# A recommendation tower's gathers, each with a wait of its own, and both gram fills of a tile in a row

## Chip, cores and metric

The kernel runs on one core of a Trainium2 chip. The metric is the device time of one execution in microseconds (us), smaller is better. Engines are named as in the profile: PE (TensorE matmul), PEld (TensorE weight load), DVE (VectorE), ACT (ScalarE), POOL (GpSimd), SP (SyncE).

## What is computed

2048 samples, 26 embedding tables of 128 columns, a dense vector of 128 columns. In short, cut from the reference:

```python
e = jnp.stack([tbl_0[ids[:, 0]], ..., tbl_25[ids[:, 25]]], axis=1)     # 2048 x 26 x 128
sd = jnp.einsum('bfd,bd->bf', e, dense)                                # 26 dots with the dense vector
ss = jnp.einsum('bfd,bgd->bfg', e, e)                                  # all pairs of features
z = jnp.concatenate([dense, sd, ss[:, iu, ju]], axis=1)                # upper triangle: 325 pairs
h = jnp.concatenate([z, dense], axis=1)
h = jnp.maximum(h @ W_top1 + b_top1, 0.0)                              # 607 -> 512
h = jnp.maximum(h @ W_top2 + b_top2, 0.0)                              # 512 -> 256
y = h @ W_top3                                                         # 256 -> 1
```

All in fp32.

## The kernel before, in words

The batch is cut into 16 tiles of 128 samples; two tiles make a step `d` of 256 samples, so there are 8 steps. For each tile the kernel needs `vecT`: for every sample its 27 vectors (26 looked up, 1 dense), with the 128 columns on the partitions. They come from two places.

**Tables that PE looks up.** Nine small tables (a tenth in three of the steps) are held in SBUF, split into two fp32r parts. PE spreads the ids (`spread_ids`, L576), DVE compares them with row numbers and so makes a one-hot "pack" (`set_pack`, L356; two packs for a table, a ring of six), and PE multiplies each pack with the table (`lookup`, L602, 8 matmuls a pack). ACT drains the sum into `vecT` (L428). `pack_done` counts packs that PE has finished: 150 in all.

**Tables that are gathered.** The other 17 (16 in the steps with ten lookups) come by POOL's indirect DMAs (L321), 128 rows each, 266 in all, in groups of four a tile, into `rows`, which holds two tiles. PE transposes a group (`transpose_rows`, L615) into one of two PSUM banks `vec_bank`, ACT copies it to `vecT` (L436). `vec_filled` counts what PE has put into `vec_bank`: row groups and gram fills alike.

**The gram.** For each sample PE multiplies its 26 vectors with its 26 vectors (`gram`, L629): two fills of `vec_bank` a tile (h = 0, 1), each 64 matmuls of 26 columns, which the profile records as 128 matmuls and 128 weight loads. ACT drains each fill (L445). DVE turns the result (L366, L372), PE transposes it (L643), ACT drains it (L452). Then comes the tower: layer 1 (L650, L654), layer 2 (L663), layer 3 (L669), one step of 256 samples at a time, in units that are drained by ACT (L460, L471).

The order on PE is written out by hand. In tiles 0 to 13, at the head of a tile, it is: gram fill 0, a unit of layer 1 or 2 of the step before, one pack of the next step's lookups, gram fill 1, another unit, another pack; then the other packs, with the row groups of the next tile between them. `gram` waits, for h = 0, for the last lookup sum, the dense vectors and the last row group of its tile. Tiles 14 and 15 are written out at the end of the program. ACT's program has the same order for its drains.

POOL's gathers of a group wait until the rows that they replace were transposed (`vec_filled`) and, from group 3 on, until the gram fills of the tile two before are done. On top of these, `gate_on_packs` (L306) makes every second gather or so wait for `pack_done`, from a small table of "packs ahead". In tile 1 and after, such waits stand on 9 gathers of a tile.

Of the kernel before, what the change touches and what calls it, by code (L numbers as in the profile page):

```python
# [19 lines left out]
TEN_STEPS = [3, 5, 7]  # L20
LATE_SPLIT = 4
GRAM_AHEAD_OF = 3
FIRST_PACKS_AHEAD = [{8: 1, 10: 2, 12: 3, 14: 4, 16: 5}, {0: 6, 2: 9, 4: 11, 6: 14, 8: 15, 10: 18, 12: 18, 14: 19, 16: 20}]
PACKS_AHEAD = [{0: 2, 2: 4, 4: 5, 6: 7, 8: 8, 10: 9, 12: 9, 14: 10, 16: 10},
               {0: 11, 2: 13, 4: 15, 6: 17, 8: 18, 10: 18, 12: 18, 14: 19, 16: 19}]
SPLIT_AT_FIRST = len(LOOKED_UP) - LATE_SPLIT


# [33 lines left out]
def build(nc, dense_t, ids, ids_t, tables, weights, y):  # L62
# [3 lines left out]
    TD = 2  # L66
# [18 lines left out]
    FG = 4  # L85
# [70 lines left out]
    def group(j):  # L156
        return GATHERED[FG * j:FG * (j + 1)]
# [4 lines left out]
    with ctx:  # L162
# [6 lines left out]
        def sem(name):  # L169
            return ctx.enter_context(nc.semaphore(name))  # L170
# [77 lines left out]
        vec_filled, vec_drained = sem("vec_filled"), sem("vec_drained")  # L248
# [6 lines left out]
        pack_set, pack_done = sem("pack_set"), sem("pack_done")  # L255
# [40 lines left out]
        @block.gpsimd  # L296
        def _(pool):
            nc.gpsimd.memset(ident[:], 0.0).then_inc(ident_zero, 1)
            for c in heights:
                nc.gpsimd.iota(row_i[c][:], pattern=[[1, c]], base=0, channel_multiplier=c  # L300
                               ).then_inc(rows_numbered, 1)
            pool.wait_ge(ident_zero, 1)
            nc.gpsimd.affine_select(out=ident[:], in_=ident[:], compare_op=ALU.not_equal, fill=1.0, base=0,
                                    pattern=[[-1, P]], channel_multiplier=1).then_inc(ident_set, 1)

            def gate_on_packs(tile, n):  # L306
                ahead = (FIRST_PACKS_AHEAD if tile < TD else PACKS_AHEAD)[tile % TD].get(n, 0)
                packs = pack_at(tile // TD, 0) + ahead
                if ahead:
                    pool.wait_ge(pack_done, packs)  # L310

            pool.wait_ge(ids_loaded, 16)
            for tile in range(TILES):
                for j in range(groups(tile)):
                    if tile >= TD:
                        pool.wait_ge(vec_filled, rows_at(same_rows(tile, j)[-1], j) + 1)
                    if tile >= TD and j == GRAM_AHEAD_OF:
                        pool.wait_ge(vec_filled, gram_at(tile - TD, 1) + 1)
                    for n, f in enumerate(group(j)):
# [82 lines left out]
        def _(act):  # L402
# [37 lines left out]
            def drain_gram(tile, h):  # L440
                use = gram_at(tile, h)
                if h == 0 and tile:
                    act.wait_ge(tile_turned, tile)
                act.wait_ge(vec_filled, use + 1)
                nc.scalar.copy(dots[:, h * HALF:(h + 1) * HALF, :],  # L445
                               vec_bank[use % 2][:, 0:HALF * GC].rearrange("p (i f) -> p i f", f=GC)
                               ).then_inc(vec_drained, 1)
# [15 lines left out]
            def drain_layer1(d, m):  # L463
                drain_unit(layer1_at(d, m), h1, m, b1_sb, 0, DS)

            def drain_layer2(d, m):
                drain_unit(layer2_at(d, m), h2, m, b2_sb, 0, DS)

            def drain_y(use, d, t0, nt):
                act.wait_ge(work_filled, use + 1)  # L470
                nc.scalar.copy(y_by_tile[:, TD * d + t0:TD * d + t0 + nt, :],  # L471
                               work_bank[use % 2][:, 0:nt * BL].rearrange("p (t i) -> p t i", t=nt)
                               ).then_inc(work_drained, 1)
# [21 lines left out]

            for tile in range(TILES - 2):
                d, t = tile // TD, tile % TD
                for h in range(2):
                    drain_gram(tile, h)
                    if t == 0 and d:  # L500
                        drain_layer1(d - 1, 1 + h)
                    if t == 1 and d and h == 0:
                        drain_layer2(d - 1, 1)
                    if t == 1 and d and h == 1:
                        drain_y(layer3_at(d - 1), d - 1, 0, TD)
                    drain_table(d + 1, half_packs(d + 1) * t + h)
# [62 lines left out]
        def _(pe):  # L569
# [49 lines left out]
            def gram(tile, h):  # L619
                into = gram_at(tile, h)  # L620
                if h == 0:
                    pe.wait_ge(sum_drained, sum_at(tile // TD + 1, 0))
                    pe.wait_ge(x_copied, tile // TD + 1)
                    pe.wait_ge(vec_drained, rows_at(tile, groups(tile) - 1) + 1)
                free_vec(into)
                for i in range(HALF):
                    for j in range(4):
                        s = BL * j + h * HALF + i
                        last = nc.tensor.matmul(vec_bank[into % 2][BL * j:BL * j + GC, i * GC:(i + 1) * GC],  # L629
                                                vecT[:, slot(tile), s, 0:GC], vecT[:, slot(tile), s, 1:VECS],  # L630
                                                start=True, stop=True)
                last.then_inc(vec_filled, 1)
# [70 lines left out]

            for tile in range(TILES - 2):
                d, t = tile // TD, tile % TD
                for h in range(2):
                    gram(tile, h)
                    if t == 0 and d:
                        layer1(d - 1, 1 + h)
                    if t == 1 and d and h == 0:  # L710
                        layer2(d - 1, 1)
                    if t == 1 and d and h == 1:
                        layer3(d - 1)
                    table_step(d + 1, half_packs(d + 1) * t + h)
                for k in range(2, half_packs(d + 1)):
                    table_step(d + 1, half_packs(d + 1) * t + k)
                    if k in ROWS_AFTER and ROWS_AFTER[k] < groups(tile + 1):
                        transpose_rows(tile + 1, ROWS_AFTER[k])
                    if t == 0 and d and k == LATE_LAYER1_AFTER:
                        layer1(d - 1, M1 - 1)  # L720
                    if k == PAIRS_AFTER:
                        transpose_pairs(tile)
                if t == 0 and d:
                    layer2(d - 1, 0)
                if t == 1:
                    if d == 0:
                        pe.wait_ge(w1x_summed, 1)
                    layer1(d, 0)
# [100 lines left out]
```

## Time and profile before

| | |
|---|---|
| median of 3 runs | 369.99 us (368.86 to 370.70) |
| the profiled execution | 371.11 us, of which the span of the profile is 369.3 us |
| granted TensorE clock, mean | 0.991 |
| PE / PEld busy | 343.2 / 313.1 us |
| DVE / ACT / POOL busy | 230.5 / 189.4 / 257.5 us |
| DMA | 26.85 MB, 73 GB/s on the mean |

A row of the timeline merges instructions of one kind that follow each other: start in us, duration in us, engine, line, operation, tiles, shape, count, and in brackets the idle time of the engine before it with what ended it. "issue" is idle time in which the engine waited for nothing that the profile shows.

### The profile page before, as it was taken

The numbers are of one execution on the slowest core, as the hardware profiler recorded it, in microseconds if no ns is written. First come the engines' busy times: TensorE is split into PE (matmuls) and PEld (weight loads), VectorE is DVE, ScalarE is ACT, GpSimd is POOL, SyncE is SP. The second block draws the span as 40 slices with busy tenths as digits, with TensorE's granted clock in tenths as the row PEclk, the third lists the DMA queues.
The fourth block names the chain that finished last, engine by engine and source line by source line (L and its number), as shares of the span: only waits on it lengthen the run. The fifth ranks groups of instructions, "written<-read, shape, count | busy, mean of one in ns | idle before, by whom it ended". The sixth has DMA issues, their size and how long they took to land.

```text
span 369.3 us, 13778 instructions
## 1 busy us (share of the span) xinstructions
PE 343.2 (93%) x6224; PEld 313.1 (85%) x6224; DVE 230.5 (62%) x324; ACT 189.4 (51%) x283; POOL 257.5 (70%) x273
## 2 busy tenths in 40 slices
PE   2997878999999999999999999999989999999976
PEld 1887768989989898989989898888979889898875
DVE  5798888866839294774849294693928468342030
ACT  1386774544637264644637265453736347372723
POOL 5788777777777777777777777777777777777000
PEclk9998998999999999999999999999999999999999
DMA  7993253222222222222222222222221222222000
GB/s 207 257 236 86 60 179 134 56 52 59 66 58 54 53 73 52 57 56 53 71 54 55 57 67 58 54 53 59 64 60 52 55 60 63 60 52 53 7 5 2
DMA packets 11756, 26.85 MB, mean 73 GB/s; under 512 B 4652, under 2 KB 5804, under 8 KB 11570
## 3 DMA queue, kind: packets, MB, share of 16 engines
q0 software_dynamic: 8512, 17.45, 18.8%
q1 hardware_dynamic: 3186, 8.52, 8.2%
q8 instruction: 49, 0.80, 1.0%
q14 instruction: 9, 0.07, 0.1%
HBM read 25.95 MB, written 0.01 MB: 70 GB/s over the span
## 4 chain that ended last, share of the span: by engine, by line
PE 86%; issue 4%; DMA 4%; POOL 2%; ACT 2%; DVE 1%; SPq 0%; ACTq 0%
PE sum_bank L602 35%; PE vec_bank L629 14%; PE work L654 11%; PE vec_bank L615 7%; PE work L663 7%; PE work L650 4%; POOL rows L321 2%; PE id_bank L576 2%; DMA rows<-in_tbl,ids_all 2%; DMA w_all<-in_tbl 2%; PE work L643 2%; PE sum_bank L598 1%; PE work L739 1%; PE work L669 1%; DVE onehot L356 1%
## 5 line engine op out<-in xcount | busy, mean ns | idle before, releaser
L321 POOL DMA_INDIRECT rows<-in_tbl,ids_all x266 | 256.7, 965 | 82.8 <-issue 68.9
L356 DVE TENSOR_TENSOR onehot<-id_bank,row_f 125x1024 fp32r<-125x1024 f32 x150 | 174.5, 1215 | 91.8 <-PE sum_bank L602 48.3
L602 PE MATMUL sum_bank<-onehot,parts 125*128 125x256 f32 x1152 | 168.1, 292 | 0.3 <-issue 0.3
L602 PEld LDWEIGHTS sum_bank<-onehot,parts 125*128 125x128 f32 x1152 | 151.3, 192 | 4.0 <-issue 0.7
L436 ACT COPY vecT<-vec_bank 128x512 f32<-128x512 f32 (+1 forms) x74 | 84.8, 1149 | 19.0 <-PE vec_bank L615 18.6
L428 ACT COPY vecT<-sum_bank 128x256 f32<-128x256 f32 x75 | 52.3, 697 | 41.0 <-PE sum_bank L602 27.9
L629 PE MATMUL vec_bank<-vecT 128*26 128x26 f32 x4096 | 53.3, 192 | 7.8 <-issue 2.6
L629 PEld LDWEIGHTS vec_bank<-vecT 128*26 128x26 f32 x4096 | 43.9, 103 | 19.5 <-issue 14.4
L460 ACT ACTIVATE late<-work,w_all 128x256 f32<-128x256 f32 (+1 forms) x50 | 22.8, 457 | 50.4 <-PE work L654 30.7
L445 ACT COPY late<-vec_bank 128x416 f32<-128x416 f32 x32 | 16.2, 506 | 58.5 <-PE vec_bank L629 58.5
L366 DVE STREAM_TRANSPOSE late<-late 128x832 f32<-128x832 f32 x16 | 29.4, 1838 | 25.4 <-ACT late L445 25.4
L615 PE MATMUL vec_bank<-ident,rows 128*128 128x128 f32 x266 | 42.3, 278 | 2.8 <-DMA rows<-in_tbl,ids_all 2.8
L654 PE MATMUL work<-late,w_all 126*128 126x256 f32 (+1 forms) x192 | 44.2, 366 | 0.0
L654 PEld LDWEIGHTS work<-late,w_all 126*128 126x128 f32 x192 | 34.8, 190 | 4.5
L615 PEld LDWEIGHTS vec_bank<-ident,rows 128*128 128x128 f32 x266 | 31.8, 142 | 3.6 <-DMA rows<-in_tbl,ids_all 3.2
L663 PE MATMUL work<-late,w_all 128*128 128x256 f32 x112 | 27.1, 386 | 0.3 <-ACT late L460 0.2
L663 PEld LDWEIGHTS work<-late,w_all 128*128 128x128 f32 x112 | 20.2, 189 | 3.5 <-issue 0.7
L576 PE MATMUL id_bank<-idsT,pick 128*128 128x512 f32 x38 | 18.4, 491 | 4.6 <-DVE idsT L380 4.6
L650 PE MATMUL work<-xT,w_all 128*128 128x256 f32 (+1 forms) x64 | 19.9, 392 | 0.2
L372 DVE COPY late<-late 128x6 f32<-128x6 f32 (+2 forms) x144 | 16.5, 198 | 1.5
L598 PE MATMUL sum_bank<-onehot,w_all 125*128 125x256 f32 x48 | 12.4, 416 | 2.5 <-DMA w_all<-in_tbl 2.5
L598 PEld LDWEIGHTS sum_bank<-onehot,w_all 125*128 125x128 f32 x48 | 10.0, 213 | 4.7 <-issue 3.2
(40 smaller groups left out, 104.3 us busy)
## 6 DMA issues: line engine op xcount, KB each, us to landing
rows<-in_tbl,ids_all POOLq DMA_INDIRECT x266, 2.6
late<-in_tbl SPq DMA_DIRECT2D x7, 480.0 KB
w_all<-in_weights SPq DMA_DIRECT2D x1, 1571.0 KB, 7.5
w_all<-in_tbl SPq DMA_DIRECT2D x3, 480.0 KB
xT<-in_dense_t SPq DMA_DIRECT2D x8, 128.0 KB
vecT<-in_ids_t SPq DMA_DIRECT2D x1, 256.0 KB, 2.8
late<-in_weights SPq DMA_DIRECT2D x1, 256.0 KB, 7.8
ids_all<-in_ids SPq DMA_DIRECT2D x1, 208.0 KB, 2.4
```

What stands on the lines that cost most here:

```text
L321: nc.gpsimd.indirect_dma_start(rows[:, tile % TD, FG * j + n, :], None, tables[f], bass.IndirectOffsetOnAxis(ids_all[:, tile, f:f + 1], 0) ...
L356: nc.vector.tensor_tensor(onehot[:, use % RING, 0:width, :], bass.AP(got.tensor, got.offset, [got.ap[0], [0, width], [1, DS]]), bass.AP(nu ...
L366: nc.vector.transpose(turned.rearrange("p c i -> p (c i)"), dots.rearrange("p i c -> p c i")).then_inc(tile_turned, 1)
L428: nc.scalar.copy(step_vec(d, place(LOOKED_UP[n] + 1)), sum_bank[use % 2][:, 0:DS].rearrange("p (t s) -> p t s", t=TD)).then_inc(sum_draine ...
L436: nc.scalar.copy(vecT[:, slot(tile), :, spot:spot + n].rearrange("d s v -> d v s"), vec_bank[use % 2][:, 0:n * P].rearrange("d (v s) -> d ...
L598: last = nc.tensor.matmul(into_sum, uncut[n - SPLIT_AT_FIRST][:, (c0 + c) * DIM:(c0 + c + 1) * DIM], hot.bitcast(fp32), start=first, stop= ...
L602: last = nc.tensor.matmul(into_sum, parts[:, k, CH_AT[n] + c0 + c, :], hot, start=first and k == 0, stop=final and k == PARTS - 1)
L615: last = nc.tensor.transpose(vec_bank[into % 2][:, n * P:(n + 1) * P], rows[:, tile % TD, FG * j + n, :], ident[:])
L629: last = nc.tensor.matmul(vec_bank[into % 2][BL * j:BL * j + GC, i * GC:(i + 1) * GC], vecT[:, slot(tile), s, 0:GC], vecT[:, slot(tile), s ...
L650: nc.tensor.matmul(out, w1x[:, cols], xT[:, d % 2, s0:s0 + ns], start=True, stop=False)
L654: last = nc.tensor.matmul(out, w1p[:, b, cols], pairsT[0:KP, b, s0:s0 + ns], start=False, stop=(b == KT - 1))
L663: last = nc.tensor.matmul(work_bank[use % 2][:, 0:ns], w2_sb[:, b, m * P:(m + 1) * P], h1[:, b, s0:s0 + ns], start=(b == 0), stop=(b == M1 ...
```

## The change

`gate_on_packs` and its two small tables go. In their place stands `GATES`, one entry for each of the 266 gathers: the counter (`PACKS` is `pack_done`, `FILLS` is `vec_filled`) and the value that it waits for, empty for the first eight. And in tiles 0 to 13 both gram fills, and both of their drains, stand directly behind each other at the tile's head.

```diff
-FIRST_PACKS_AHEAD = [{8: 1, 10: 2, 12: 3, 14: 4, 16: 5}, {0: 6, 2: 9, 4: 11, 6: 14, 8: 15, 10: 18, 12: 18, 14: 19, 16: 20}]
-PACKS_AHEAD = [{0: 2, 2: 4, 4: 5, 6: 7, 8: 8, 10: 9, 12: 9, 14: 10, 16: 10},
-               {0: 11, 2: 13, 4: 15, 6: 17, 8: 18, 10: 18, 12: 18, 14: 19, 16: 19}]
+PACKS, FILLS = 0, 1
+GATES = [
...
+    [(FILLS, 23), (FILLS, 24), (PACKS, 43), (PACKS, 44), (PACKS, 45), (FILLS, 26), (FILLS, 26), (FILLS, 27),
+     (FILLS, 27), (FILLS, 27), (PACKS, 46), (FILLS, 28), (PACKS, 47), (PACKS, 48), (PACKS, 49), (FILLS, 30),
+     (PACKS, 51)],
...
+]
...
-            def gate_on_packs(tile, n):
-                ahead = (FIRST_PACKS_AHEAD if tile < TD else PACKS_AHEAD)[tile % TD].get(n, 0)
-                packs = pack_at(tile // TD, 0) + ahead
-                if ahead:
-                    pool.wait_ge(pack_done, packs)
+            def keep_behind_pe(what=None, count=0):
+                if count:
+                    pool.wait_ge([pack_done, vec_filled][what], count)
...
-                        gate_on_packs(tile, FG * j + n)
+                        keep_behind_pe(*GATES[tile][FG * j + n])
...
             for tile in range(TILES - 2):
                 d, t = tile // TD, tile % TD
+                drain_gram(tile, 0)
+                drain_gram(tile, 1)
                 for h in range(2):
-                    drain_gram(tile, h)
...
             for tile in range(TILES - 2):
                 d, t = tile // TD, tile % TD
+                gram(tile, 0)
+                gram(tile, 1)
                 for h in range(2):
-                    gram(tile, h)
```

What the change moves on PE, at the head of tile 3, where units of layer 2 (L663) and layer 3 (L669) of the step before stand between the gram fills (L629; L602 is a pack's lookup, L615 the last row group). Before:

```order
L602 MATMUL sum_bank<-onehot,parts 128x256 x8
L615 MATMUL vec_bank<-ident,rows 128x128
L663 MATMUL work<-late,w_all 128x256 x4
L629 MATMUL vec_bank<-vecT 26x26 x64
L663 MATMUL work<-late,w_all 128x256 x4
L602 MATMUL sum_bank<-onehot,parts 128x256 x8
L629 MATMUL vec_bank<-vecT 26x26 x64
L669 MATMUL work<-late,w_all 32x64 x8
L602 MATMUL sum_bank<-onehot,parts 128x256 x8
```

With the change (L646 is the lookup, L659 the row group, L707 layer 2, L673 the gram, L713 layer 3):

```order
L646 MATMUL sum_bank<-onehot,parts 128x256 x8
L659 MATMUL vec_bank<-ident,rows 128x128
L707 MATMUL work<-late,w_all 128x256 x4
L673 MATMUL vec_bank<-vecT 26x26 x128
L707 MATMUL work<-late,w_all 128x256 x4
L646 MATMUL sum_bank<-onehot,parts 128x256 x8
L713 MATMUL work<-late,w_all 32x64 x8
L646 MATMUL sum_bank<-onehot,parts 128x256 x8
```

Nothing is added or left out on PE; the second fill now comes ahead of a unit and a pack.

On POOL, the first nine gathers of tile 4 with the semaphores that they wait for. Before, every second one waits:

```order
L321 DMA rows<-in_tbl_1,ids_all 128x128 [waits pack_done,vec_filled]
L321 DMA rows<-in_tbl_2,ids_all 128x128
L321 DMA rows<-in_tbl_3,ids_all 128x128 [waits pack_done]
L321 DMA rows<-in_tbl_5,ids_all 128x128
L321 DMA rows<-in_tbl_8,ids_all 128x128 [waits pack_done,vec_filled]
L321 DMA rows<-in_tbl_11,ids_all 128x128
L321 DMA rows<-in_tbl_12,ids_all 128x128 [waits pack_done]
L321 DMA rows<-in_tbl_13,ids_all 128x128
L321 DMA rows<-in_tbl_14,ids_all 128x128 [waits pack_done,vec_filled]
```

With the change each of them does, on whichever counter its entry names:

```order
L364 DMA rows<-in_tbl_1,ids_all 128x128 [waits vec_filled]
L364 DMA rows<-in_tbl_2,ids_all 128x128 [waits vec_filled]
L364 DMA rows<-in_tbl_3,ids_all 128x128 [waits pack_done]
L364 DMA rows<-in_tbl_5,ids_all 128x128 [waits pack_done]
L364 DMA rows<-in_tbl_8,ids_all 128x128 [waits pack_done,vec_filled]
L364 DMA rows<-in_tbl_11,ids_all 128x128 [waits vec_filled]
L364 DMA rows<-in_tbl_12,ids_all 128x128 [waits vec_filled]
L364 DMA rows<-in_tbl_13,ids_all 128x128 [waits vec_filled]
L364 DMA rows<-in_tbl_14,ids_all 128x128 [waits vec_filled]
```

The order of the gathers is the same; their waits are.

## Rows read from the trace of the kernel before

**Rows 1.** The page: busy time, share of the span, instructions, of PE, PEld and POOL

```profile
PE 343.2 (93%) x6224; PEld 313.1 (85%) x6224; DVE 230.5 (62%) x324; ACT 189.4 (51%) x283; POOL 257.5 (70%) x273
```

**Rows 2.** The page: the chain that ended last, by engine

```profile
PE 86%; issue 4%; DMA 4%; POOL 2%; ACT 2%; DVE 1%; SPq 0%; ACTq 0%
```

**Rows 3.** The page's groups: busy, mean ns of one, idle before and what ended it

```profile
L321 POOL DMA_INDIRECT rows<-in_tbl,ids_all x266 | 256.7, 965 | 82.8 <-issue 68.9
...
L629 PE MATMUL vec_bank<-vecT 128*26 128x26 f32 x4096 | 53.3, 192 | 7.8 <-issue 2.6
```

**Rows 4.** Waits: engine, line, releaser; us in total, times, longest

```profile
POOL rows L321 <- PE sum_bank L602: 8.2, 27, 0.3
...
PEld vec_bank L629 <- issue: 14.4, 51, 1.3
```

**Rows 5.** The page: PE's instruction queue; packets, MB, share

```profile
q8 instruction: 49, 0.80, 1.0%
```

**Rows 6.** Timeline of PEld, tile 15's gram fills and what follows

```profile
350.33 1.18 PEld L629 LDWEIGHTS vec_bank<-vecT 128*26 128x26 f32 x128 [0.37 <-issue]
351.54 0.30 PEld L650 LDWEIGHTS work<-xT,w_all 128*128 128x128 f32 x2
351.76 0.75 PEld L654 LDWEIGHTS work<-late,w_all 126*128 126x128 f32 x6
352.63 0.21 PEld L629 LDWEIGHTS vec_bank<-vecT 128*26 128x26 f32 x17
354.03 1.01 PEld L629 LDWEIGHTS vec_bank<-vecT 128*26 128x26 f32 x111 [1.20 <-issue]
355.08 0.30 PEld L650 LDWEIGHTS work<-xT,w_all 128*128 128x128 f32 x2
355.30 0.75 PEld L654 LDWEIGHTS work<-late,w_all 126*128 126x128 f32 x6
355.97 0.53 PEld L774 LDWEIGHTS sum_bank<-xT,w_all 128*128 128x128 f32 x4
356.42 0.53 PEld L774 LDWEIGHTS id_bank<-xT,w_all 128*128 128x128 f32 x4
356.87 0.19 PEld L739 LDWEIGHTS work<-late,w_all 128*128 128x128 f32 x1
357.94 0.86 PEld L739 LDWEIGHTS work<-late,w_all 128*128 128x128 f32 x7 [0.89 <-issue]
```

**Rows 7.** Windows there: busy (count) by engine, PEclk, DMA share, GB/s last

```profile
351.30:351.60 0.30, 0.30 (x38) 0.26 (x25) 0.00 (x0) 0.00 (x0) 0.00 (x0) 1.00 0.00 0
351.60:352.10 0.50, 0.50 (x6) 0.50 (x6) 0.00 (x0) 0.38 (x1) 0.00 (x0) 1.00 0.12 33
...
355.10:355.60 0.50, 0.50 (x10) 0.50 (x5) 0.00 (x0) 0.39 (x1) 0.00 (x0) 1.00 0.16 33
```

**Rows 8.** Timeline of PE, head of tile 3

```profile
100.35 1.71 PE L629 MATMUL vec_bank<-vecT 128*26 128x26 f32 x128
102.00 1.99 PE L663 MATMUL work<-late,w_all 128*128 128x256 f32 x8
103.64 1.30 PE L602 MATMUL sum_bank<-onehot,parts 125*128 125x256 f32 x8
104.87 2.02 PE L629 MATMUL vec_bank<-vecT 128*26 128x26 f32 x128
106.70 0.46 PE L669 MATMUL work<-late,w_all 128*32 128x64 f32 x16
```

**Rows 9.** Timeline of PEld, long idle times near fills in tiles 1, 11 and 12

```profile
65.56 0.61 PEld L629 LDWEIGHTS vec_bank<-vecT 128*26 128x26 f32 x63 [0.64 <-issue]
...
276.25 0.26 PEld L669 LDWEIGHTS work<-late,w_all 128*32 128x32 f32 x12 [0.83 <-issue]
...
296.00 0.30 PEld L650 LDWEIGHTS work<-xT,w_all 128*128 128x128 f32 x2 [1.01 <-issue]
```

**Rows 10.** Timeline: POOL's last gather of tile 6; PEld, the transposes that need it

```profile
155.21 0.94 POOL L321 DMA_INDIRECT rows<-in_tbl,ids_all  x1 [0.30 <-issue]
...
158.19 0.47 PEld L615 LDWEIGHTS vec_bank<-ident,rows 128*128 128x128 f32 x4
```

**Rows 11.** Timeline: POOL's eleventh gather of tile 4; time to landing of all gathers

```profile
106.53 0.94 POOL L321 DMA_INDIRECT rows<-in_tbl,ids_all  x1 [0.30 <-issue]
...
DMA to landing us min/median/max: 2.4/2.6/6.5
```

**Rows 12.** Timeline: the table copies of tile 0 on ACT and DVE, and PE's wait behind them

```profile
42.76 1.02 ACT L415 COPY work<-w_all 125x1024 f32<-125x1024 f32 x1
...
49.19 1.23 DVE L341 TENSOR_TENSOR parts<-work,parts 125x1024 fp32r<-125x1024 f32 x1 [0.91 <-ACT parts L409]
...
55.47 0.85 PE L643 MATMUL work<-ident,late 128*126 128x128 f32 x3 [2.60 <-DVE late L372]
```

**Rows 13.** Windows: columns as in Rows 7

```profile
50.00:55.00 5.00, 2.88 (x24) 2.59 (x21) 4.97 (x11) 3.41 (x5) 3.78 (x5) 1.00 0.77 244
55.00:60.00 5.00, 4.53 (x24) 4.35 (x24) 5.00 (x9) 2.22 (x4) 3.78 (x5) 0.66 0.62 236
...
350.00:355.00 5.00, 3.70 (x266) 3.32 (x264) 0.00 (x0) 1.43 (x5) 0.00 (x0) 1.00 0.01 3
```

More of the change, by code:

```diff
@@ L22 @@
 GRAM_AHEAD_OF = 3
-FIRST_PACKS_AHEAD = [{8: 1, 10: 2, 12: 3, 14: 4, 16: 5}, {0: 6, 2: 9, 4: 11, 6: 14, 8: 15, 10: 18, 12: 18, 14: 19, 16: 20}]
-PACKS_AHEAD = [{0: 2, 2: 4, 4: 5, 6: 7, 8: 8, 10: 9, 12: 9, 14: 10, 16: 10},
-               {0: 11, 2: 13, 4: 15, 6: 17, 8: 18, 10: 18, 12: 18, 14: 19, 16: 19}]
+PACKS, FILLS = 0, 1
+GATES = [
+    [(), (), (), (), (), (), (), (), (PACKS, 1), (PACKS, 1), (PACKS, 2), (PACKS, 3), (PACKS, 3), (FILLS, 1),
+     (PACKS, 5), (PACKS, 6), (FILLS, 2)],
+    [(PACKS, 9), (FILLS, 3), (PACKS, 12), (PACKS, 13), (FILLS, 4), (PACKS, 15), (PACKS, 16), (PACKS, 17),
+     (PACKS, 18), (PACKS, 18), (FILLS, 6), (PACKS, 19), (PACKS, 19), (FILLS, 7), (PACKS, 20), (FILLS, 8),
+     (PACKS, 23)],
+    [(FILLS, 9), (FILLS, 10), (PACKS, 25), (PACKS, 25), (PACKS, 25), (PACKS, 25), (PACKS, 26), (FILLS, 11),
+     (FILLS, 12), (FILLS, 12), (FILLS, 13), (PACKS, 28), (PACKS, 28), (FILLS, 14), (PACKS, 30), (PACKS, 31),
+     (PACKS, 32)],
+    [(PACKS, 33), (FILLS, 17), (PACKS, 34), (FILLS, 18), (FILLS, 19), (FILLS, 19), (FILLS, 19), (FILLS, 20),
+     (FILLS, 20), (PACKS, 37), (FILLS, 21), (FILLS, 21), (FILLS, 21), (PACKS, 39), (FILLS, 22), (PACKS, 40),
+     (PACKS, 40)],
+    [(FILLS, 23), (FILLS, 24), (PACKS, 43), (PACKS, 44), (PACKS, 45), (FILLS, 26), (FILLS, 26), (FILLS, 27),
+     (FILLS, 27), (FILLS, 27), (PACKS, 46), (FILLS, 28), (PACKS, 47), (PACKS, 48), (PACKS, 49), (FILLS, 30),
+     (PACKS, 51)],
+    [(FILLS, 31), (PACKS, 52), (FILLS, 32), (FILLS, 33), (FILLS, 33), (FILLS, 33), (FILLS, 34), (FILLS, 34),
+     (PACKS, 55), (PACKS, 55), (FILLS, 35), (FILLS, 35), (PACKS, 56), (FILLS, 36), (PACKS, 58), (PACKS, 58),
+     (FILLS, 37)],
+    [(PACKS, 60), (PACKS, 61), (PACKS, 62), (FILLS, 39), (FILLS, 40), (PACKS, 64), (PACKS, 64), (FILLS, 41),
+     (FILLS, 41), (FILLS, 41), (PACKS, 65), (FILLS, 42), (PACKS, 66), (FILLS, 43), (PACKS, 68), (FILLS, 44)],
+    [(PACKS, 70), (PACKS, 71), (PACKS, 71), (FILLS, 46), (PACKS, 74), (PACKS, 74), (PACKS, 74), (FILLS, 47),
+     (FILLS, 47), (PACKS, 75), (PACKS, 75), (FILLS, 48), (FILLS, 48), (PACKS, 76), (FILLS, 49), (PACKS, 78)],
+    [(PACKS, 78), (PACKS, 79), (FILLS, 50), (FILLS, 51), (PACKS, 81), (FILLS, 52), (PACKS, 83), (PACKS, 83),
+     (PACKS, 83), (FILLS, 53), (FILLS, 53), (PACKS, 84), (PACKS, 84), (FILLS, 54), (PACKS, 86), (FILLS, 55),
+     (PACKS, 87)],
+    [(FILLS, 56), (FILLS, 57), (PACKS, 90), (FILLS, 58), (FILLS, 59), (FILLS, 59), (FILLS, 59), (FILLS, 60),
+     (FILLS, 60), (PACKS, 93), (PACKS, 93), (FILLS, 61), (FILLS, 61), (PACKS, 94), (FILLS, 62), (PACKS, 96),
+     (PACKS, 96)],
+    [(PACKS, 97), (PACKS, 98), (FILLS, 64), (PACKS, 99), (FILLS, 65), (FILLS, 66), (PACKS, 102),
+     (PACKS, 102), (FILLS, 67), (FILLS, 67), (FILLS, 67), (PACKS, 103), (FILLS, 68), (FILLS, 68),
+     (PACKS, 104), (FILLS, 69)],
+    [(PACKS, 106), (FILLS, 70), (FILLS, 71), (PACKS, 109), (FILLS, 72), (PACKS, 111), (PACKS, 112),
+     (PACKS, 112), (PACKS, 112), (FILLS, 73), (FILLS, 73), (PACKS, 113), (FILLS, 74), (FILLS, 74),
+     (FILLS, 74), (PACKS, 114)],
+    [(FILLS, 75), (PACKS, 116), (PACKS, 116), (FILLS, 76), (FILLS, 77), (PACKS, 119), (PACKS, 119),
+     (FILLS, 78), (PACKS, 121), (PACKS, 121), (FILLS, 79), (FILLS, 79), (FILLS, 79), (PACKS, 122),
+     (FILLS, 80), (FILLS, 80), (PACKS, 123)],
+    [(FILLS, 81), (PACKS, 125), (FILLS, 82), (FILLS, 83), (PACKS, 128), (PACKS, 129), (PACKS, 130),
+     (FILLS, 85), (FILLS, 85), (FILLS, 86), (FILLS, 86), (FILLS, 86), (PACKS, 131), (PACKS, 131),
+     (FILLS, 87), (FILLS, 87), (PACKS, 132)],
+    [(FILLS, 88), (PACKS, 134), (PACKS, 134), (PACKS, 135), (PACKS, 136), (FILLS, 90), (PACKS, 137),
+     (FILLS, 91), (FILLS, 92), (PACKS, 140), (PACKS, 140), (PACKS, 140), (FILLS, 93), (FILLS, 93),
+     (PACKS, 141), (FILLS, 94)],
+    [(FILLS, 94), (PACKS, 143), (FILLS, 95), (PACKS, 145), (FILLS, 96), (FILLS, 97), (PACKS, 147),
+     (FILLS, 98), (PACKS, 149), (PACKS, 150), (PACKS, 150), (FILLS, 99), (FILLS, 99), (FILLS, 99),
+     (FILLS, 100), (FILLS, 100)],
+]
```

## The prediction

> **What bounds the kernel now.** I read the page first. PE is busy 343.2 of 369.3 us [rows 1], and 86% of the chain that ended last is PE's [rows 2]: what lengthens PE's work lengthens the kernel, nearly one for one. Then the groups and the waits. POOL is a steady stream, 0.94 us busy and 0.30 us between gathers, and none of its waits on PE is over 0.3 us [rows 3, 4], which is the same 0.30 that stands ahead of a gather without a wait: no gate holds it today. The row to look at is a third one: PEld idled 14.4 us in 51 places inside the gram, "issue", the longest 1.3 us [rows 4]. Nothing that the profile shows held it there, so I went for PE's own instructions.
>
> PE and PEld record 6224 + 6224 = 12448 instructions [rows 1]; PE's instruction queue brought 49 packets, 0.80 MB [rows 5], one for 254 of them (256 with the waits between). A gram fill is 128 matmuls and 128 loads, so **one fill eats one packet**. Tile 15 shows what that does, because the gathers are over by then and the only transfers are instructions. Its first fill starts at 350.33 [rows 6]; transfers are at zero until 351.60, then 33 GB/s for 0.5 us, which is one packet of 16 KB [rows 7]; 17 loads into the second fill PEld stops for 1.20 us and goes on at 354.03 [rows 6], 2.4 us after the packet began. From there 111 + 2 + 6 + 4 + 4 + 1 = 128 loads pass, with their matmuls 256 instructions, and it stops again, 0.89 us, until 357.94 [rows 6]; that packet came in the window from 355.10 [rows 7]. So a packet is asked for about 1.1 to 1.3 us after the last border is crossed, is there some 2.5 us later, and two borders crossed at full speed cannot lie closer than 3.7 to 3.9 us.
>
> Elsewhere PE keeps clear of this, since between the two fills stand a unit and a pack: in tile 3 the second fill starts 4.5 us after the first [rows 8]. The stall shows only where a border falls badly: 0.64, 0.83, 1.01 us [rows 9], and twice smaller (0.26 and 0.48 us by the same view).
>
> **The gram fills, the large term.** 14 tiles now run 512 instructions without a pause. Such a stretch holds exactly two borders, 256 instructions or one fill's time apart, today 1.65 us [rows 8]. The second must wait for its packet. Tile 15 gives the length: from the first fill's start to the go-on 3.7 us; without the unit between, the border would lie 25 loads into the second fill, 103 loads remain, and at the 1.67 us of a mean fill (53.3 / 32, [rows 3]) these are 1.3 us: 5.0 us for the pair. Where the border lies later, the packet is asked for later and less remains, so I take 4.9 for all. Today a pair takes 1.65 + 1.83 = 3.5 us [rows 8], 3.4 on the mean. Plus 1.5 us by 14 is **+21.0**. The five stalls of today in these tiles go with it, 0.64 + 0.83 + 1.01 + 0.26 + 0.48: **-3.2**. One entry into and one exit from the small shape are saved a tile; no row has two fills in a row. The first fill shows 0.37 us idle ahead of its loads, most of it after a drain [rows 6], which would be 14 x 0.37 = 5.2 at most, and 0 at least; in tile 3 PE shows no idle time ahead of either fill [rows 8], so I take **-1.0**. In tile 13 the count puts the first border at the very head of the pair, hence a third one right behind its end, 1.7 us after the go-on where 3.7 are needed: **+2.0**.
>
> Here a rule speaks against me. The Trainium skill ("Runtime: NRT & Kernel Launch", Instruction fetch mechanics) gives PE's instruction memory as 2048 instructions, refilled in blocks of 256 while the current one runs, the cost of a border mostly hidden. By that a burst of 512 would be covered and this whole term would be zero. It also calls the memory two lines of one block each, which is what tile 15 looks like; the two sentences disagree, and [rows 6] decide for the second.
>
> **Behind the fills.** In tile 0 ACT's copy of a table, at 42.76 us, moves behind the drain of the second fill, some 2.9 us later; DVE waits for it (0.91 us already) and PE for DVE, 2.60 us [rows 12]. PE itself comes 1.5 later, so its wait grows by what is over, less DVE's slack: **+0.4**. In the other tiles ACT has each fill drained in 0.5 us, and the units behind wait for nothing new: 0.
>
> **The gates.** A gather's new event lies 0.35 to 3.9 us before its start in the order of today, so with the old order they would bind nowhere. The move spoils some: gather 11 of tile 4 starts at 106.53 [rows 11] and waits for pack 46, the one at the head of tile 3, whose matmuls end at 103.64 + 1.30 = 104.94 [rows 8]; this pack now stands behind the second fill, 1.7 us later in PE's order before any stall. POOL then slips up to 1 us, a tile or so at a time, and since its stream has no reserve (17 x 1.25 = 21.2 us a tile, as PE's), what it loses counts where the margin is small, at the row groups that PE transposes. That is tiles 4 and 6: the last gather of tile 6 starts at 155.21, lands 2.6 us later [rows 11], 157.8, and the transposes start at 158.19 [rows 10]: 0.4 us. I take 0.5 us at each, **+1.0**. Bounds: 0 (the stalls slow PE and give POOL time), and 3 if four tiles have it at 0.75 each. The waits themselves cost nothing, since the 0.30 us ahead of a gather are there with and without one [rows 3, 4]. Behind a gather's wait stand only gathers, so PE's transposes are the only ones who can feel it.
>
> **The clock.** In the 5 us after PE's 2.60 us wait in tile 0 the granted clock is 0.66; after tile 15's 1.20 us stall it stays at 1.00 [rows 13]. The new stalls, 1.3 to 2.3 us, lie between. A stretch at 0.66 loses (1 - 0.66) x 5 = 1.7 us at most, none where PE is held by instructions. Ends: 0, and 14 x 1.7 = 24. Nearest is the row at 1.20, so I take little, **+2.0**.
>
> Sum: 21.0 - 3.2 - 1.0 + 2.0 + 0.4 + 1.0 + 2.0 = 22.2. The profiled execution took 371.1; 393.3 then, and 1.1 less against the median of the runs: **392 us**.
>
> **Rivals.** (A) PE fetches further ahead than tile 15 makes me think (there the program's end is near): the stalls do not come, only the gates' 1.0 and tile 0's 0.4 are left, 371.4 us. The rule above says so; for it, most of the 49 borders pass unseen; against it, the stops exactly 256 instructions apart. 0.08. (B) Faster: the fills gain by their neighbourhood. Nothing stalls, the entry is saved, 14 x 0.37 = 5.2, and the 3.2 of today go: 371.1 - 8.4 + 1.4 - 1.1 = 363 us. It decides if a packet is there within 1.65 us of the one before; tile 15's took 3.7. 0.05. (C) The clock drops behind half of the stalls or more: 14 x 1.7 / 2 = 12 in place of 2, 402 us, and 414 if behind all. 0.15. (D) No stalls, but the gates bind: their 3 us with tile 0's 0.4, 373 us. 0.04. My forecast has 0.68, with a range of its own from 384 to 399: a pair between 4.4 and 5.3 us.
>
> **Numbers.** Half a per cent is about what a measurement of this kernel can tell from no change. Slower: 0.68 + 0.15 + 0.04 = 0.87; within half a per cent, A: 0.08; faster, B: 0.05. The range runs from 380 to 406: it holds the forecast and most of C, and leaves out A, B, D (0.17) and the far end of C. Its lower end is a pair at 4.1 us in place of 4.9 (14 x 0.8 = 11).
>
> **What would show it.** In the profile of the changed kernel: PEld's idle time at the gram with "issue" behind it goes from 14.4 us to 30 or more, with 14 stops of 1.2 to 2.3 us, one in each of the tiles 0 to 13, each in or after the second half of the pair; the number of instruction packets stays 49; POOL shows waits on PE over 0.3 us, as now the gates hold it to PE's pace; a window at a clock under 1.00 behind some stalls. I am wrong if a pair of fills takes under 4 us, or if the stops are there but another wait of PE shrinks by as much.

## The result, and the profile after

| | before | after |
|---|---|---|
| median | 369.43 us (4 runs, 367.38 to 370.70) | 388.18 us (4 runs, 387.75 to 389.83) |
| the profiled execution | 371.11 us, span 369.3 us | 387.89 us, span 386.1 us |
| granted clock, mean | 0.991 | 0.981 |
| PE / PEld busy | 343.2 / 313.1 us | 347.5 / 316.1 us |

The changed kernel takes 1.052 times the time of the one before (1.0491 to 1.0548): slower, as forecast. The forecast was 392 us with a range of 380 to 406. The profiled execution has 16.8 us more span, where the sum had 22.2; the medians lie 18.8 us apart, since the execution profiled before is 1.7 us above its median.

From the page of the changed kernel: the chain by engine, the groups of the gathers, of the gram's matmuls and loads and of the transposes, and PE's instruction queue.

```profile
PE 84%; issue 7%; DMA 3%; POOL 1%; ACT 1%; DVE 1%; SPq 0%; ACTq 0%
...
L364 POOL DMA_INDIRECT rows<-in_tbl,ids_all x266 | 256.2, 963 | 101.4 <-issue 65.2
...
L673 PE MATMUL vec_bank<-vecT 128*26 128x26 f32 x4096 | 53.9, 192 | 21.7 <-issue 16.1
L673 PEld LDWEIGHTS vec_bank<-vecT 128*26 128x26 f32 x4096 | 44.5, 103 | 34.6 <-issue 32.0
...
L659 PE MATMUL vec_bank<-ident,rows 128*128 128x128 f32 x266 | 41.7, 275 | 0.3 <-DMA rows<-in_tbl,ids_all 0.3
...
q8 instruction: 49, 0.80, 0.9%
```

Against [rows 2], "issue" has gone from 4% of the chain to 7%. Against [rows 3], the gram's matmuls are busy as long as before, 53.9 us for 53.3; what grew is the idle time ahead of them, 7.8 to 21.7 us, with "issue" 2.6 to 16.1 of it. The packets are still 49 [rows 5]: nothing was added, the same instructions come in another order. From the waits of the changed kernel (us in all, times, longest):

```profile
PEld vec_bank L673 <- issue: 32.0, 76, 1.7
...
POOL rows L364 <- PE sum_bank L646: 29.0, 34, 4.4
...
PE vec_bank L673 <- issue: 16.1, 14, 1.6
```

PEld's 14.4 us [rows 4] have become 32.0. The second row looks as alarming as the first: POOL now waits for PE up to 4.4 us, where before no wait was over 0.3. Experiment 1 says which of the two is cause and which effect. The timelines show the stop itself, first PE's at the head of tile 3:

```profile
101.78 1.89 PE L707 MATMUL work<-late,w_all 128*128 128x256 f32 x8
103.60 3.27 PE L673 MATMUL vec_bank<-vecT 128*26 128x26 f32 x214
107.68 0.54 PE L673 MATMUL vec_bank<-vecT 128*26 128x26 f32 x42 [0.81 <-issue]
108.15 1.99 PE L707 MATMUL work<-late,w_all 128*128 128x256 f32 x8
```

214 matmuls run, then PE holds for 0.81 us with 42 to go. The pair takes 108.15 - 103.60 = 4.55 us, where the fills of [rows 8] take 1.65 + 1.83. In tile 2 it is worse; this is PEld's timeline:

```profile
80.02 1.18 PEld L673 LDWEIGHTS vec_bank<-vecT 128*26 128x26 f32 x107 [0.33 <-issue]
81.39 0.30 PEld L673 LDWEIGHTS vec_bank<-vecT 128*26 128x26 f32 x22 [0.19 <-issue]
81.89 0.60 PEld L673 LDWEIGHTS vec_bank<-vecT 128*26 128x26 f32 x55 [0.20 <-issue]
82.66 0.29 PEld L673 LDWEIGHTS vec_bank<-vecT 128*26 128x26 f32 x20 [0.17 <-issue]
83.13 0.25 PEld L673 LDWEIGHTS vec_bank<-vecT 128*26 128x26 f32 x16 [0.19 <-issue]
84.81 0.39 PEld L673 LDWEIGHTS vec_bank<-vecT 128*26 128x26 f32 x36 [1.43 <-issue]
```

Two kinds of idle time stand in this view, both called "issue": the short ones of 0.17 to 0.20 us, which the kernel before has too, and one long one, 1.43 us, in the pair. PE's row of the waits has the long ones almost alone, 16.1 us, so about half of PEld's 32.0 is of the short kind. Only the long ones are new. There is one in the pair of each of the tiles 0 to 13; by the distance from the last matmul's start to the next one's they are 0.29 to 1.83 us, 18.0 in all (tile 13's, the 0.29, is as short as the short kind and is known by its place alone). Tile 13 has one more, right behind its pair:

```profile
330.66 0.73 PEld L673 LDWEIGHTS vec_bank<-vecT 128*26 128x26 f32 x74 [0.21 <-issue]
331.56 0.31 PEld L673 LDWEIGHTS vec_bank<-vecT 128*26 128x26 f32 x22 [0.16 <-issue]
332.04 0.36 PEld L673 LDWEIGHTS vec_bank<-vecT 128*26 128x26 f32 x30 [0.17 <-issue]
332.44 0.30 PEld L707 LDWEIGHTS work<-late,w_all 128*128 128x128 f32 x2
334.12 1.16 PEld L707 LDWEIGHTS work<-late,w_all 128*128 128x128 f32 x6 [1.39 <-issue]
```

The short stop at 330.66 is the second border. Behind it 74 + 22 + 30 + 2 = 128 loads pass, with their matmuls 256 instructions, and PEld stops again, in the first loads of layer 2.

The trace also records the transfers of PE's instruction queue one by one, and they tie the stops to the packets directly. At each of the 14 long stops (tiles 0 to 12, and the one behind tile 13's pair) a packet of 16 KB started 2.2 to 2.7 us before PE went on and had landed 1.2 to 1.5 us before it; the next packet started 1.1 to 1.6 us after. In none of the 14 pairs do two packets start closer together than 3.2 us.

### The profile page after: what moved, and what is told of

It is laid out like the page before. It is cut to its first block, busy times and chain, and to the rows that moved or that the text cites. A ratio compares the mean times of both kernels' runs of the same rounds, so it can differ in the third digit from the quotient of the medians.

```text
span 386.1 us, 13778 instructions
## 1 busy us (share of the span) xinstructions
PE 347.5 (90%) x6224; PEld 316.1 (82%) x6224; DVE 230.4 (60%) x324; ACT 189.0 (49%) x283; POOL 257.0 (67%) x273
## 4 chain that ended last, share of the span: by engine, by line
PE 84%; issue 7%; DMA 3%; POOL 1%; ACT 1%; DVE 1%; SPq 0%; ACTq 0%
PE sum_bank L646 33%; PE vec_bank L673 14%; PE work L698 11%; PE vec_bank L659 7%; PE work L707 7%; PE work L694 4%; PE id_bank L620 2%; PE sum_bank L642 2%; DMA rows<-in_tbl,ids_all 2%; DMA w_all<-in_tbl 2%; PE work L687 2%; POOL rows L364 1%; PE work L784 1%; PE work L713 1%; DVE onehot L399 1%
## 5 line engine op out<-in xcount | busy, mean ns | idle before, releaser
L646 PE MATMUL sum_bank<-onehot,parts 125*128 125x256 f32 x1152 | 168.5, 293 | 1.4 <-issue 1.4
L646 PEld LDWEIGHTS sum_bank<-onehot,parts 125*128 125x128 f32 x1152 | 151.8, 193 | 5.5 <-issue 2.0
L479 ACT COPY vecT<-vec_bank 128x512 f32<-128x512 f32 (+1 forms) x74 | 84.8, 1150 | 16.8 <-PE vec_bank L659 16.4
L673 PE MATMUL vec_bank<-vecT 128*26 128x26 f32 x4096 | 53.9, 192 | 21.7 <-issue 16.1
L673 PEld LDWEIGHTS vec_bank<-vecT 128*26 128x26 f32 x4096 | 44.5, 103 | 34.6 <-issue 32.0
L698 PE MATMUL work<-late,w_all 126*128 126x256 f32 (+1 forms) x192 | 46.4, 379 | 0.0
L659 PE MATMUL vec_bank<-ident,rows 128*128 128x128 f32 x266 | 41.7, 275 | 0.3 <-DMA rows<-in_tbl,ids_all 0.3
L698 PEld LDWEIGHTS work<-late,w_all 126*128 126x128 f32 x192 | 36.6, 199 | 5.3
L659 PEld LDWEIGHTS vec_bank<-ident,rows 128*128 128x128 f32 x266 | 31.4, 141 | 1.0 <-DMA rows<-in_tbl,ids_all 0.5
L707 PE MATMUL work<-late,w_all 128*128 128x256 f32 x112 | 27.3, 386 | 1.2 <-issue 1.0
L707 PEld LDWEIGHTS work<-late,w_all 128*128 128x128 f32 x112 | 20.2, 189 | 4.2 <-issue 1.4
L415 DVE COPY late<-late 128x6 f32<-128x6 f32 (+2 forms) x144 | 16.5, 204 | 1.5
```

Source lines behind the costliest of these rows:

```text
L479: nc.scalar.copy(vecT[:, slot(tile), :, spot:spot + n].rearrange("d s v -> d v s"), vec_bank[use % 2][:, 0:n * P].rearrange("d (v s) -> d ...
L646: last = nc.tensor.matmul(into_sum, parts[:, k, CH_AT[n] + c0 + c, :], hot, start=first and k == 0, stop=final and k == PARTS - 1)
L659: last = nc.tensor.transpose(vec_bank[into % 2][:, n * P:(n + 1) * P], rows[:, tile % TD, FG * j + n, :], ident[:])
L698: last = nc.tensor.matmul(out, w1p[:, b, cols], pairsT[0:KP, b, s0:s0 + ns], start=False, stop=(b == KT - 1))
L707: last = nc.tensor.matmul(work_bank[use % 2][:, 0:ns], w2_sb[:, b, m * P:(m + 1) * P], h1[:, b, s0:s0 + ns], start=(b == 0), stop=(b == M1 ...
```

## The experiments

### 1 and 2: the fills alone, the gates alone

The change is two edits, so each was made by itself. Experiment 1 is the kernel before with the fills next to each other (and their drains on ACT the same way) and the old gates:

```
+                gram(tile, 0)
+                gram(tile, 1)
                 for h in range(2):
-                    gram(tile, h)
```

> The old gates, and only the move of the fills. Theory (PE's instruction packets: two borders 256 instructions apart cannot be crossed within less than 3.2 to 4.0 us): all of the loss is here, 386 to 390 us, one stop of 0.3 to 1.8 us in each of the tiles 0 to 13. Rival (the gates hold POOL and so PE): under 375 us.

Measured: 387.74 us (385.25 to 390.35), ratio 1.0528 (1.0471 to 1.0585). Its waits:

```profile
PEld vec_bank L630 <- issue: 33.1, 76, 1.7
...
POOL rows L321 <- PE sum_bank L603: 20.7, 27, 4.2
...
PE vec_bank L630 <- issue: 16.7, 14, 1.6
```

Experiment 2 is the changed kernel with the fills back in their old places:

```
-                gram(tile, 0)
-                gram(tile, 1)
                 for h in range(2):
+                    gram(tile, h)
```

> The new gates, and the fills in their old places. Theory: 369 to 371 us, no wait of POOL on PE over 0.5 us, the fills' idle time with issue behind it as before, 14 to 15 us. Rival (gates): 375 us and more.

Measured: 369.85 us (368.15 to 370.56), ratio 1.0012 (0.9992 to 1.0032). Its waits:

```profile
PEld vec_bank L672 <- issue: 14.4, 50, 1.4
...
POOL rows L364 <- PE sum_bank L645: 7.1, 22, 0.7
```

The fills alone give all of the loss, the gates alone none. The gates do bind now and then, by 0.7 us where 0.5 was the most expected, and the median doesn't show it. Its profile has one wait of PE for gathers that the kernel before hasn't, 1.6 us at 116.6 us, for tile 4's rows:

```profile
PE vec_bank L658 <- DMA rows<-in_tbl,ids_all: 1.9, 2, 1.6
```

POOL's gathers of that group started no later than before, and PE was 1 us ahead of its old time, so this row doesn't say that a gate made it. POOL's long waits are in experiment 1 as well, with the old gates: they are the effect. PE is late, and either set of gates then holds the gathers to PE's pace. That is harmless, since PE waits for gathers only 0.3 us in the changed kernel.

### 3 and 4: how far apart must the fills be?

If two borders cannot be crossed within 3.7 us or so, the loss must shrink with the work that stands between the fills. Experiment 3 puts the unit of layer 1 or 2 between them (some 1.9 us), experiment 4 the lookup pack (some 1.2 us), both from the last load of one fill to the first of the next; the kernel before has both. In 3:

```
                 for h in range(2):
+                    if h == 0:
+                        gram(tile, 0)
...
+                    if h == 0:
+                        gram(tile, 1)
                     table_step(d + 1, half_packs(d + 1) * t + h)
```

> As the changed kernel, but the unit of layer 1 or 2 (1.6 us) stands between the two fills in tiles 2 to 13; both packs and the other unit behind. Theory: the second border comes 1.65 + 1.6 = 3.25 us after the first instead of 1.65, so stops shrink to 0 to 0.7 us, and with tiles 0 and 1 still adjacent the time is 373 to 378 us. Rival (it is the neighbourhood of the fills as such that costs): 370 us, since no fills are neighbours in 12 of 14 tiles. Rival (what costs is that both fills come before both packs, so that DVE or ACT is late): 385 us or more.

Measured: 373.56 us (372.03 to 376.68), ratio 1.0106 (1.0071 to 1.0141). In 4 `table_step` and the unit change places:

```
                 gram(tile, 0)
-                gram(tile, 1)
                 for h in range(2):
+                    table_step(d + 1, half_packs(d + 1) * t + h)
+                    if h == 0:
+                        gram(tile, 1)
```

> As the changed kernel, but the first pack's lookup (1.2 us) stands between the two fills, the units behind. Theory: borders 2.85 us apart, stops of 0.3 to 1.1 us in all 14 tiles: 376 to 381 us, more than with the unit between and less than with nothing. Neighbourhood rival: 370 us.

Measured: 375.24 us (373.98 to 375.64), ratio 1.0157 (1.0124 to 1.019), just under the range expected. PEld in tile 3, first with the unit between, then with the pack:

```profile
103.77 1.62 PEld L709 LDWEIGHTS work<-late,w_all 128*128 128x128 f32 x8
105.72 0.99 PEld L675 LDWEIGHTS vec_bank<-vecT 128*26 128x26 f32 x79 [0.33 <-issue]
107.08 0.70 PEld L675 LDWEIGHTS vec_bank<-vecT 128*26 128x26 f32 x49 [0.36 <-issue]
```

```profile
101.87 1.00 PEld L647 LDWEIGHTS sum_bank<-onehot,parts 125*128 125x128 f32 x8
103.00 0.97 PEld L674 LDWEIGHTS vec_bank<-vecT 128*26 128x26 f32 x79
105.05 0.50 PEld L674 LDWEIGHTS vec_bank<-vecT 128*26 128x26 f32 x49 [1.07 <-issue]
```

The border lies at the same load of the fill, behind the 79th, and the stop there is 0.36 us with 1.9 us of work between the fills, 1.07 with 1.2. So the stop goes with the distance. That the kind of work doesn't matter is not shown, since no run has the two at one distance. Experiment 3's 373.56 is not all stops: its tiles 0 and 1, where there is no unit yet, have 1.27 and 2.14 us, and in the execution profiled PE also waited 3.2 us for gathers.

### 5: adjacent, but half as long

```
-                for i in range(HALF):
+                for i in range(HALF // 2):
```

> The changed kernel with every fill cut to the first 32 of its 64 matmuls (the other samples' grams are left out), still two fills in a row. The pair is now 256 instructions, so it can hold one border and not two. Packet theory: the pair takes 1.5 to 1.8 us and the stops of 1.0 to 1.7 us are gone, but for one or two tiles where a border lies at its very edge. Neighbourhood rival (two fills in a row are slow by themselves, whatever they hold): half of the loss per pair is left, 0.6 us and more in each of 14 tiles. The time itself says little here: the gathers' stream alone, 266 by 1.25 us and the tail, gives 350 to 360 us.

Measured: 361.67 us, one run. PEld's timeline of tile 2:

```profile
75.34 1.28 PEld L673 LDWEIGHTS vec_bank<-vecT 128*26 128x26 f32 x112 [0.33 <-issue]
76.78 0.27 PEld L673 LDWEIGHTS vec_bank<-vecT 128*26 128x26 f32 x16 [0.15 <-issue]
77.08 0.30 PEld L694 LDWEIGHTS work<-xT,w_all 128*128 128x128 f32 x2
```

The two fills are as close as in the changed kernel, and in tiles 0 to 13 they run through in 1.66 to 1.99 us, without a long stop in any of them. It is not two fills meeting that costs, nor the PSUM banks or drains, but 512 short instructions in a row. Half of the gram's work saves only 7.3 us against the 369.0 of the kernel before on the same chip (350 to 360 us was expected for the gathers alone), since now the gathers are the bound; one row of the waits says it:

```profile
PE vec_bank L659 <- DMA rows<-in_tbl,ids_all: 21.9, 17, 2.4
```

### 6: the same pairs, the borders moved

The changed kernel, with waits that are long fulfilled put ahead of PE's work; the 127 more that are written make 63 instructions more in the trace.

```
-            pe.wait_ge(pick_set, 1)
+            for _ in range(128):
+                pe.wait_ge(pick_set, 1)
```

> The changed kernel with 63 more waits (long fulfilled) on PE at the program's start, so that every packet border comes 63 instructions earlier in the work. Packet theory: each stop moves by 63 instructions, 31 or 32 loads: in tile 2 from 37 loads before the end of the pair to 68 or 69 before it, in tile 6 from load 185 of the pair to load 153. Tile 9 gets what tile 13 had, a stop right behind the pair, and tile 13 loses it; in tiles 10 to 13 a second stop comes in. 386 to 393 us. Any rival whose cause is in the data, banks or transfers of the tile leaves the stops where they were.

Measured: 393.66 us, one run, 0.7 above the range expected and 5.5 above the changed kernel's median. The added waits themselves are 2.5 us of it: PE's first idle time is 8.6 us in place of 4.7, and the first pair starts at 41.19 in place of 38.74. PEld in tile 2 and in tile 13:

```profile
82.29 0.58 PEld L673 LDWEIGHTS vec_bank<-vecT 128*26 128x26 f32 x53 [0.19 <-issue]
84.25 0.78 PEld L673 LDWEIGHTS vec_bank<-vecT 128*26 128x26 f32 x68 [1.39 <-issue]
85.08 0.30 PEld L694 LDWEIGHTS work<-xT,w_all 128*128 128x128 f32 x2
...
335.41 0.30 PEld L673 LDWEIGHTS vec_bank<-vecT 128*26 128x26 f32 x29 [1.78 <-issue]
335.74 2.13 PEld L707 LDWEIGHTS work<-late,w_all 128*128 128x128 f32 x8
```

In tile 2 the stop now has 68 loads behind it instead of 36: 32 loads earlier, for 63 instructions. In tile 13 the extra stop behind the pair is gone and the pair has a long one. Tile 9 got what tile 13 lost:

```profile
240.01 0.79 PEld L673 LDWEIGHTS vec_bank<-vecT 128*26 128x26 f32 x70 [0.57 <-issue]
240.98 0.56 PEld L673 LDWEIGHTS vec_bank<-vecT 128*26 128x26 f32 x54 [0.18 <-issue]
241.58 0.73 PEld L707 LDWEIGHTS work<-late,w_all 128*128 128x128 f32 x4
243.74 0.73 PEld L707 LDWEIGHTS work<-late,w_all 128*128 128x128 f32 x4 [1.43 <-issue]
```

70 + 54 + 4 = 128 loads again. Of the second stops expected in tiles 10 to 13 one came, 0.71 us in tile 11. The stop follows the count of instructions and no semaphore, bank or transfer of the kernel's own. This is the firmest evidence of the study.

### 7 to 9: the other way, can less burst gain?

If bursts cost, spreading the fills should pay. Experiment 7 takes the kernel before and cuts each fill in half with the work of its `h` between the halves:

```
-                    gram(tile, h)
+                    gram(tile, h, (0,))
...
+                    if d:
+                        gram(tile, h, (1,))
                     table_step(d + 1, half_packs(d + 1) * t + h)
```

> The kernel before, old gates and old order, but each fill is cut in two halves of 128 instructions with the unit (1.6 us) between them. Packet theory: no two borders are closer than 3.3 us anywhere in tiles 2 to 13, so what stops the kernel before still has there (0.5, 0.8, 1.0 us) goes, and each half starts with instructions that are already queued, which saves up to 0.2 us a fill: 363 to 368 us. Rival (entering and leaving the small shape costs): 24 more entries at 0.1 to 0.3 us eat it, 369 to 374 us.

Measured: 369.0 us (367.72 to 370.66), ratio 1.0 (0.9978 to 1.0022): a miss, and the lower end of what the rival, dear entries into the fills, had. Part of the reason is that in odd tiles the work between the halves is layer 3, 32 instructions in some 0.4 us, which parts nothing; stops of 0.64, 0.72 and 0.91 us remain. Experiment 8 moves the second fill of the kernel before, whole, behind both units and both packs:

```
                     table_step(d + 1, half_packs(d + 1) * t + h)
+                    if h == 1:
+                        gram(tile, 1)
```

> The other way from the change: the kernel before with the second fill put behind both units and both packs (5.6 us after the first fill's end in tiles 2 to 13, 2.4 us in tiles 0 and 1). Packet theory: the stops of tiles 0 and 1 shrink from 0.35 and 0.7 us to 0 to 0.3; those in tiles 9 and 11 to 13 come from a border at the very edge of a single fill and stay or move; so 367.5 to 369.5 us, at most 1 us better. Rival (distance between fills is worth something by itself, the more the better): 366 us or less.

Measured: 368.89 us (367.27 to 370.2), ratio 0.9993 (0.9972 to 1.0014). Here the expectation was wrong on the stops: in tiles 0 to 13 not one is left, and still the median doesn't move. Experiment 9 repairs 7: the halves of the odd tiles' second fill now have the pack between them.

```
+                    if d and not (t and h):
+                        gram(tile, h, (1,))
+                    table_step(d + 1, half_packs(d + 1) * t + h)
+                    if not d or t and h:
+                        gram(tile, h, (1,))
```

> As e8_split, but in the odd tiles the second fill's halves have the pack's lookup (1.2 us) between them in place of layer 3, which is 32 instructions in 0.4 us and so parted nothing. Packet theory: with 1.2 to 1.6 us between all halves in tiles 0 to 13 their stops, 2.8 us in e8_split's profile for these tiles, fall under 1 us in all, and the time is 366 to 368 us. Rival (the extra entries cost what the stops give back, and the gathers' pace holds PE): 368.5 to 371 us.

Measured: 367.47 us (366.19 to 369.21), ratio 0.9967 (0.9945 to 0.9989). Its timeline on PE in tile 3:

```profile
101.75 0.73 PE L630 MATMUL vec_bank<-vecT 128*26 128x26 f32 x64
102.41 1.22 PE L602 MATMUL sum_bank<-onehot,parts 125*128 125x256 f32 x8
103.56 0.73 PE L630 MATMUL vec_bank<-vecT 128*26 128x26 f32 x64
104.22 1.22 PE L602 MATMUL sum_bank<-onehot,parts 125*128 125x256 f32 x8
```

It is the fastest kernel of the study that does all the work, with one stop of 0.98 us left ahead of tile 14, by 0.3%: the interval leaves out 1, but this is within what I called no difference. It has as many entries into fills as experiment 7, which speaks against them as what held that one back. The kernels that keep whole fills, in order of what stands between the two of a tile:

| between the two fills | stops, tiles 0 to 13 | median |
|---|---|---|
| nothing (after) | 19.3 us | 388.18 us |
| pack, some 1.2 us | 11.4 us | 375.24 us |
| unit, some 1.9 us | 6.9 us | 373.56 us |
| unit and pack, some 2.9 us (before) | 3.8 us | 369.43 us |
| both units and packs | 0 | 368.89 us |

The stops are start to start, one execution each, those of tiles 14 and 15 left out. The medians come from several chips; the kernel before took 369.0 to 369.4 us on each. From before to after the stops grow by 15.5 us and the median by 18.8; down from before, 3.8 us of stops bring at most 1. That last step stays unexplained: the stops of before may have lain where PE had a wait coming in any case, but no run tells.

## Why the prediction was right, step by step

**What bounds.** Right. PE's time is the kernel's time, nearly one for one, and PE's own instructions were what to look at.

**A fill eats one packet, and two borders need 3.7 to 3.9 us.** Right, and shown: stops 128 loads apart (the changed kernel, experiment 6), moved by the count (6), gone with half the instructions (5), graded by the distance (3, 4). Over the pairs of the changed kernel two packets start 3.2 to 4.0 us apart, wider than tile 15 alone gave. Counted in the work, 128 loads back from the stop, two borders were as close as 2.3, 3.1 and 2.2 us in tiles 11 to 13, whose first border lies within the first 20 loads of the pair: there the first packet started within 0.5 us of that border, where in tiles 0 to 10 it came 0.8 to 1.6 us behind it. The prediction's "cannot lie closer than 3.7 to 3.9" was too strict, and why a border at a pair's head is dealt with sooner was not tried.

**A pair of 4.9 us, +21.0.** Right in kind, a little too large. The 14 pairs take 3.63 to 5.42 us, 66.1 in all, 4.72 on the mean. The two fills of a tile took 49.6 before, the stops inside them counted: +16.5. The stops of before that lay outside fills, 0.48 and 0.83, are gone as well: +15.2 for what the sum had as 21.0 - 3.2 - 1.0 = 16.8. The short pairs are those whose first border lies early or late: tile 11 took 3.63, tile 13 3.99. I had taken 4.9 for all. My sign of being wrong, a pair under 4 us, came in these two, and the stops of 1.2 to 2.3 us were that long in 10 of the 14 pairs; so the mechanism was right, and its size, which I had taken as the same for all pairs, was not.

**The entry saved, -1.0.** The measurement doesn't separate it. At the head of tile 2's pair PEld still shows its 0.33 us.

**Tile 13's third border, +2.0.** There, behind the end of the pair as counted, 1.39 us in place of 2.0.

**Tile 0, +0.4.** Wrong, by little: PE's wait for DVE did not grow.

```profile
56.53 0.55 PE L687 MATMUL work<-ident,late 128*126 128x128 f32 x3 [2.58 <-DVE late L415]
```

It was 2.60 [rows 12]. What PE lost in the pair and behind it, DVE's chain lost too, so the two moved together.

**The gates, +1.0.** Right that they bind (0.7 us in experiment 2, without the stops), wrong that it costs: in tiles 4 and 6 the transposes wait for nothing; in the whole kernel PE waits 0.3 us for gathers, by the same view 2.8 before, all of it ahead of the first pair in both. I gave the slower PE only as the lower bound of that term, and it is what happened: PE's stops give POOL more time than the gates take. Experiment 2 has the gates without the stops, and its median shows no cost there either, with PE's one wait of 1.6 us for gathers in tile 4 as the open end.

**The clock, +2.0.** Right in size. The windows (busy and count of PE, PEld, DVE, ACT and POOL, then PEclk, DMA share, GB/s) show it dropping behind the stops of tiles 4 and 10:

```profile
123.00:128.00 5.00, 3.47 (x214) 2.58 (x213) 1.94 (x2) 0.98 (x2) 3.78 (x5) 1.00 0.20 56
128.00:133.00 5.00, 4.69 (x61) 3.98 (x61) 0.00 (x0) 0.98 (x2) 1.49 (x2) 0.66 0.17 43
260.00:265.00 5.00, 3.11 (x228) 2.55 (x229) 1.60 (x2) 0.98 (x2) 3.78 (x5) 1.00 0.23 56
265.00:270.00 5.00, 5.00 (x69) 4.27 (x57) 0.02 (x1) 0.98 (x2) 1.06 (x2) 0.66 0.13 33
```

and once more in tile 0, at 43 us. A fourth, behind PE's wait of 2.58 us in tile 0, the kernel before [rows 13] and experiment 1 have too. The kernel before had a drop of its own that the changed one hasn't, from the end of PE's 2.2 us wait for gathers on:

```profile
30.00:35.00 5.00, 2.82 (x14) 2.82 (x14) 5.00 (x5) 2.22 (x2) 4.09 (x4) 0.67 0.27 71
```

So the changed kernel has four drops and the one before two. Experiment 1 puts a price on the three new ones, since PE's order there is the same: its profiled execution has none of these three and a span of 383.5 us at a mean clock of 0.996, the changed kernel's 386.1 at 0.981. That is 2.6 us for three drops, an estimate, since the 14 pairs differ by 0.6 us between these two as well. Its own four runs go the same way: 383.5 us at 0.996, 384.5 at 0.991, 387.3 at 0.982, 388.6 at 0.974. Rival C, which wanted a drop behind half of the stops or more, did not come; rivals A and B, no stops at all, fell, and the mean 1.65 us that B asked for between packets was never seen. D fell with them.

**The sum.** 15.2 + 1.4 + 2.6 and 0 for tile 0 and the gates make 19.2. Two terms that I hadn't make it less: the first pair starts 1.3 us earlier (38.74 for 40.01), since PE waited less for its first gathers and had no drop behind that wait, which experiment 1 shows too (39.00) with the old gates, and experiment 2 (38.86) with the old order, and tile 15's two stops, which the change doesn't touch, came to 0.95 + 0.61 in place of 1.20 + 0.89, 0.5 us less. That is 17.4; the span grew by 16.8.

The Trainium skill ("Runtime: NRT & Kernel Launch", Instruction fetch mechanics) gives PE 2048 instructions of its own memory, which would have held a burst of 512. It also describes two lines of one block, with the size that it gives most engines and not PE. The stops 128 loads apart agree with two lines; the 2048 instructions would have made rival A come true and did not.

## What to carry to other kernels

Idle time marked "issue" on an engine that nothing holds is worth a count: if the stops lie 256 instructions apart, the engine is waiting for its own code, and moving two bursts of short instructions next to each other makes it worse: here by 0.3 to 1.8 us a pair, mostly about the 3.2 to 4.0 us between two packets less what the work between the two borders takes. Keep a burst of short matmuls under one packet and put two or three microseconds of long ones between bursts; beyond that distance nothing clear of noise was gained here. And where another engine's waits grow with the change, first undo the stops before blaming its semaphores: here its new waits, up to 4.4 us, cost nothing.

## What I had not expected of the hardware

**Small pauses of PE beside gathers.** Even where no border is, a fill is cut by pauses of 0.15 to 0.21 us, "issue", as in the timeline of tile 2 above. In the kernel before and the changed one most of them begin 0.45 or 1.2 us after a gather's start on POOL, two to a gather; in experiment 9 they are less regular. In tile 15, when the gathers are over, 128 loads pass in 1.18 us without one [rows 6], where the fills of tile 3 take 1.65 and 1.83 [rows 8]. This was seen and not tried: no run took the gathers away.

**The clock drops behind some stops only.** Of the changed kernel's stops of 1.3 us and more, those of tiles 0, 4 and 10 have a drop behind them and those of tiles 2, 5 and 7 (1.5 to 1.7 us) don't; the 1.2 to 1.9 us ones of experiment 1 have none in its profiled execution and, by the mean clock, some in its other runs. Experiment 6 has no drop behind its wait of 2.6 us in tile 0, where the other kernels named here have one, and four drops elsewhere. What decides it was not found.

**Stops that cost nothing.** Experiment 8 took 3.8 us of stops away, and the median did not move.
